# Four conditioned residual layers on one core: setup and chunk loop in one program, U kept on chip, a second gather buffer, written orders for begin and end

## What is computed

```python
# layer 0: weights made per entry, low rank (K = 30)
U = (mu @ W_dec + b_dec).reshape(B, 257, 30)       # W_dec is 128 x 7710
param = einsum('bik,kj->bij', U, V)
x = x + einsum('bsd,bde->bse', x, param[:, :-1]) + param[:, -1]
# layer 1: modulated product, demodulated, clipped
x = x + clip((x * styles) @ weight.T * dcoefs + bias, -256, 256)
# layer 2: down 256 -> 64, relu, up 64 -> 256, both scaled and shifted per entry
x = x + relu(x @ w_down) @ w_up + x
# layer 3: norms with gathered gains, three side networks, a two-layer network, a norm
h = ln(ln(x, pw_g[id], pw_b[id]), cp_g[c], cp_b[c])
t = ln(x, tm_g[c], tm_b[c]); s = ln(x, ms_g[m], ms_b[m])
cat = [w0*h, w1*t, w2*(x + mem), w3*(x + noi), w4*(x + res), w5*s]
x = x + ln(silu(cat @ W1 + b1) @ W2 + b2, g, be)
```

## Time and profile before

| | |
|---|---|
| three runs | 599.15, 596.51, 599.20 us (median 599.15) |
| the profiled execution | 592.32 us |
| its span, first to last instruction | 590.5 us |
| mean granted TensorE clock | 0.943 |
| busy: PE, DVE, ACT, POOL | 507.6, 457.5, 273.3, 395.6 us |
| moved by DMA | 69.61 MB |

### The profile page before, as it was taken

The page is one execution under the profiler, slowest core; times in us unless marked ns, Lnnn a source line. Parts: engine busy times, 40 slices in busy tenths (PEclk is TensorE's granted clock), DMA queues, the critical chain, the costliest instruction groups (busy, mean ns, idle before and its releaser), DMA issues.

```text
span 590.5 us, 8825 instructions
## 1 busy us (share of the span) xinstructions
PE 507.6 (86%) x2927; PEld 374.3 (63%) x2960; DVE 457.5 (77%) x857; ACT 273.3 (46%) x445; POOL 395.6 (67%) x382
## 2 busy tenths in 40 slices
PE   4898056569999989999989998999899999989773
PEld 3896023246676767776767676777677767757553
DVE  2579324756898979898979898989798989997543
ACT  5031010635655454647473736373737373646320
POOL 8048040878687868788777868695969697886400
PEclk9799567979999999999999999999999999999896
DMA  8954443334243525261616170708080706032011
GB/s 257 374 173 134 123 109 90 77 127 99 102 123 114 136 100 144 93 172 62 163 71 192 42 214 20 230 5 227 7 231 3 231 3 180 1 109 78 31 36 36
DMA packets 41098, 69.61 MB, mean 118 GB/s; under 512 B 5113, under 2 KB 23525, under 8 KB 40692
## 3 DMA queue, kind: packets, MB, share of 16 engines
q1 hardware_dynamic: 35732, 52.46, 32.1%
q0 software_dynamic: 5344, 16.87, 7.8%
HBM read 56.51 MB, written 12.80 MB: 117 GB/s over the span
## 4 chain that ended last, share of the span: by engine, by line
PE 46%; issue 8%; POOL 7%; DMA 4%; DVE 3%; ACT 1%; POOLq 0%; DVEq 0%; ACTq 0%
PE ps_d L773 7%; PE ps_c L739 6%; PE ps_c L740 6%; PE ps_c L741 6%; DMA pw_rows<-in_pw,gidx 4%; POOL xm_t L1141 4%; PE ps_d L782 3%; PE ps_b L739 3%; PE ps_b L740 3%; PE ps_b L741 3%; POOL x3be L1193 2%; PE ps_b L808 2%; PE ps_a L808 2%; PE ps_a L792 1%; POOL h L1168 1%
## 5 line engine op out<-in xcount | busy, mean ns | idle before, releaser
L1134 POOL DMA_INDIRECT pw_rows<-in_pw,gidx x64 | 72.4, 1131 | 27.9 <-POOL gidx L1130 13.3
L773 PE MATMUL ps_d<-xm_t,l_w 128*128 128x512 f32 x128 | 62.4, 632 | 16.0 <-POOL xm_t L1141 16.0
L1168 POOL TENSOR_TENSOR h<-xhat,pw_rows 128x1024 f32<-128x1024 f32 x16 | 38.4, 2397 | 52.4 <-DMA pw_rows<-in_pw,gidx 44.5
L1141 POOL TENSOR_TENSOR xm_t<-x_t,style 128x1024 f32<-128x1024 f32 x16 | 30.4, 1902 | 39.5 <-DVE x_t L1007 39.5
L773 PEld LDWEIGHTS ps_d<-xm_t,l_w 128*128 128x128 f32 x128 | 24.4, 201 | 43.2 <-issue 41.9
L739 PE MATMUL ps_b<-w_h,act_t_l 128*128 128x256 f32 x128 | 40.6, 317 | 9.5 <-DVE act_t_l L1091 9.5
L961 ACT ACTIVATE tm_t_h<-ps_a 128x1024 fp32r<-128x1024 f32 x16 | 16.4, 1026 | 62.5 <-DVE ps_a L1070 59.0
L984 ACT ACTIVATE ps_c<-ps_c,bias_cols 128x512 f32<-128x512 f32 x32 | 19.8, 658 | 48.6 <-PE ps_c L741 48.6
L1187 POOL TENSOR_TENSOR w_up<-w_up,ugub 128x1024 f32<-128x1024 f32 x16 | 38.2, 2385 | 1.3
L792 PEld LDWEIGHTS ps_a<-act_bd,w_up 128*128 128x128 f32 x256 | 33.6, 206 | 8.0 <-issue 4.7
L1193 POOL TENSOR_TENSOR x3be<-x,ln_gb 128x1024 f32<-128x1024 f32 x16 | 38.4, 2400 | 0.4
(11 more groups left out here) (229 smaller groups left out, 1527.1 us busy)
## 6 DMA issues: line engine op xcount, KB each, us to landing
ugub<-ugub_scratch SPq DMA_DIRECT2D x32, 512.0 KB
x_t<-in_x_t SPq DMA_DIRECT2D x16, 512.0 KB, 7.5
out<-y_out SPq DMA_DIRECT2D x16, 512.0 KB, 8.8
u_scratch<-set_u_all SPq DMA_DIRECT2D x2, 1920.0 KB
u_ch<-u_scratch SPq DMA_DIRECT2D x16, 240.0 KB, 7.9
set_wdec<-in_W_dec SPq DMA_DIRECT2D x1, 1935.0 KB, 19.5
set_wdec<-in_W_dec SPq DMA_DIRECT2D x1, 1920.0 KB, 11.3
set_w<-in_int_W SPq DMA_DIRECT2D x1, 1536.0 KB, 22.4
```

Source lines behind the costliest of these rows:

```text
L773: m = eng.matmul(ps_l1[:, o, :], l1_w[:, k, o * P:(o + 1) * P], xm_t[:, k, :], start=k == 0, stop=k == KB - 1)
L1134: eng.indirect_dma_start(pw_rows[:, j, :], None, t["pw"], bass.IndirectOffsetOnAxis(ap=gidx[:, j:j + 1], axis=0)).then_inc(s_pw, 16)
L1141: eng.tensor_tensor(by_entry(xm_t[:, :, :]), by_entry(x1_t[:, :, :]), cols(style, c), ALU.mult).then_inc(g_xm, 1)
L1168: eng.tensor_tensor(h1[:, :, :], xhat[:, :, :], pw_rows[:, :, 0:D], ALU.mult).then_inc(g_h1m, 1)
```

## The change

One program takes the place of two blocks. The setup is cut into stages of its own (`pe_dec`, `v_decode`, `act_hid`, `g_dcoef`, ...), and every engine gets three lists: `begin`, where setup stages and the stages of the first chunks are mixed in a written order, `order` with lags for the loop (again five passes of two slots, slots 6 to 15, with all lags two higher on TensorE), and `end`, the last chunks in a written order. No barrier stands between setup and loop; the first chunk's stages wait for what they need of the setup (`if first(c)`).

U stays on the chip: `u_all` is laid out [feature, half, component, entry], VectorE writes it contiguously, and a new stage `act_u` copies a chunk's part into `u_ch` in the order that `pe_t` reads. Its two writes and 16 reads of memory are gone. `pw_rows` and `gidx` have two buffers, and `g_gather` waits for `g_hadd` of two chunks before; the gather's place in the list is a slot ahead of `g_hmul`. `W_dec` is loaded first, mu sixth. W1, the nets' W2 and their rows now lie in the memory of `W_dec` and are loaded when the decode is over. The decode goes round six banks where it went round four.

```diff
-    last = max(lag for _, lag in order)
-    fill = last + 2 - last % 2
+def run_slots(eng, begin, order, end, fill):
+    for stage, n in begin:
+        stage(eng, chunk(n))
     with eng.Fori(fill // 2, NCH // 2) as i:
         for k in range(2):
+            for stage, lag in order:
+                d = k - lag
+                stage(eng, Chunk(2 * i + d, i + (d - d % 2) // 2, d % 2))
+    for stage, n in end:
+        stage(eng, chunk(n))
...
-        u_all = sb("u_all", [P, KB, B, RK])
+        u_all = sb("u_all", [P, KB, RK, B])
...
+            wdec = st("wdec", [MU, D * RK])
+            w1 = wdec[:, 0:12 * D].rearrange("p (k d) -> p k d", d=D)
+            w2n = wdec[:, 12 * D:18 * D].rearrange("p (n k d) -> p n k d", n=3, d=D)
+            rown = wdec[:, 18 * D:27 * D].rearrange("p (n m d) -> p n m d", n=3, d=D)
...
+        def load_w2n(eng, c):
+            eng.wait_ge(m_dec, NG)
+            eng.dma_start(w2n.rearrange("p n k d -> p (n k) d"), feat(t["nets_W2"])).then_inc(d_w2n, 16)
...
+        def pe_dec(eng, c):
+            g = c.n
+            k, lo, hi = GROUPS[g]
+            if lo == 0:
+                eng.wait_ge(d_front, 32)
+                eng.wait_ge(d_dec[k], 16)
+            wait(eng, v_dec, g - len(dec_bank) + 1)
+            w = wdec[:, k * P * RK:(k + 1) * P * RK].rearrange("m (i r) -> m r i", r=RK)
+            for r in range(lo, hi):
+                m = eng.matmul(dec_bank[g % 6][:, (r - lo) * B:(r - lo + 1) * B], w[:, r, :], mu, start=True, stop=True)
+            m.then_inc(m_dec, 1)
...
+        def act_u(eng, c):
+            if first(c):
+                eng.wait_ge(v_dec, NG)
+            wait(eng, p_t, c.n - 1)
+            src = u_all[:, :, :, bass.ds(c.n * CB, CB)].rearrange("p k r b -> p k b r")
+            eng.activation(u_ch[c.ring][:, :, :, :], src, ACT.Copy).then_inc(a_u, 1)
...
-            wait(eng, g_h1, c.n)
-            wait(eng, s_pw, 16 * CT * c.n)
+            wait(eng, g_h1, c.n - 1)
+            wait(eng, s_pw[c.ring], 16 * CT * c.half)
...
         @block.sync
+                      begin=[(load_dec, 0), (load_bdec, 0), (load_aw, 0), (load_l1, 0), (load_front, 0),
+                             (load_dec, 1), (load_x, 0), (load_side, 0), (load_ident, 0), (load_entry, 0),
+                             (load_bias, 0), (load_late, 0), (load_ub, 0), (load_ub, 1), (load_nets, 0),
+                             (load_ids, 0), (load_weights, 0), (load_x, 1), (load_rown, 0), (load_w2n, 0),
+                             (load_w1, 0), (load_up, 0), (load_ids, 1), (load_ub, 2), (load_up, 1), (load_ub, 3),
+                             (load_x, 2), (load_up, 2), (load_x, 3), (load_ub, 4), (load_shift, 0)],
...
         @block.tensor
+                      begin=[(pe_dec, 0), (pe_dec, 1), (pe_dec, 2), (pe_dec, 3), (pe_dec, 4), (pe_dec, 5),
+                             (pe_dec, 6), (pe_tail, 0), (pe_dec, 7), (pe_dec, 8), (pe_dec, 9), (pe_dec, 10),
+                             (pe_style, 0), (pe_dec, 11), (pe_dec, 12), (pe_dec, 13), (pe_dec, 14), (pe_dec, 15),
+                             (pe_dc, 0), (pe_hid, 0), (pe_ug, 0), (pe_t, 0), (pe_mo, 0), (pe_x1, 0), (pe_l1, 0),
+                             (pe_mot, 0), (pe_t, 1), (pe_dn, 0), (pe_row, 0), (pe_up, 0), (pe_x1, 1), (pe_x3r, 0),
+                             (pe_cls, 0), (pe_l1, 1), (pe_t, 2), (pe_xht, 0), (pe_tm, 0), (pe_dn, 1), (pe_ms, 0),
+                             (pe_up, 1), (pe_x1, 2), (pe_x3r, 1), (pe_t, 3), (pe_l1, 2)],
...
+                           (pe_x3r, 15), (pe_w2, 13), (pe_shift, 14), (pe_w1_x3, 14), (pe_w1_tm, 14),
+                           (pe_xht, 15), (pe_hht, 14), (pe_ms, 15), (pe_tm, 15), (pe_w1_ms, 14), (pe_w1_h, 14),
+                           (pe_cp, 15), (pe_w2, 14), (pe_shift, 15), (pe_w1_x3, 15), (pe_w1_tm, 15),
+                           (pe_hht, 15), (pe_w1_ms, 15), (pe_w1_h, 15), (pe_w2, 15)],
...
         @block.gpsimd
+                      begin=[(g_init, 0), (g_b2rows, 0), (g_w2low, 0), (g_dcoef, 0), (g_moroot, 0), (g_style, 0),
+                             (g_gather, 0), (g_wup, 0), (g_gather, 1), (g_style, 1), (g_rootx, 0), (g_w1mlow, 0),
+                             (g_wup, 1), (g_w1xlow, 0), (g_hmul, 0), (g_w1tlow, 0), (g_hadd, 0), (g_style, 2),
+                             (g_res, 0), (g_rootx, 1), (g_rooth, 0), (g_gather, 2), (g_wup, 2), (g_hmul, 1)],
+                      order=[(g_hadd, 5), (g_style, 3), (g_res, 5), (g_rootx, 4), (g_rooth, 5), (g_wup, 3),
+                             (g_rooty, 6), (g_gather, 3), (g_hmul, 4)],
```

More of the change, by code:

```diff
@@ L55 @@
 BRW = PIECES * CB
+GROUP = 4
+GROUPS = [(k, r, min(r + GROUP, RK)) for k in range(KB) for r in range(0, RK, GROUP)]
+NG = len(GROUPS)
 EPS = 1e-5
@@ L80, in settle, with first, chunk @@
     eng.sem_inc(sem, 1)
-def run_slots(eng, order):
-    last = max(lag for _, lag in order)
-    fill = last + 2 - last % 2
[L88 to L95, removed]
+def first(c):
+    return isinstance(c.n, int) and c.n == 0
+def chunk(n):
+    return Chunk(n, n // 2, n % 2)
@@ new lines, in conditioned_residuals, with late @@
+        nets = ((w1_mem, mu, 0, MU), (w1_nr, st_nr, 0, 64), (w1_nr, st_nr, 64, 96))
+        def late(name, shape, dt=F32):
+            return ctx.enter_context(nc.sbuf_tensor(name, shape, dt, side="right"))
+        y_out = [late(f"y_out{r}", [P, CT, D]) for r in range(2)]
+        act_t_h, act_t_l = (late(f"act_t_{e}", [P, KB, CH], F32R) for e in "hl")
+        h_t_h, h_t_l = (late(f"h_t_{e}", [P, KB, CH], F32R) for e in "hl")
+        ms_t_h, ms_t_l = (late(f"ms_t_{e}", [P, KB, CH], F32R) for e in "hl")
@@ new lines, in conditioned_residuals @@
+        tm_t_h, tm_t_l = (late(f"tm_t_{e}", [P, KB, CH], F32R) for e in "hl")
+        xh_t = late("xh_t", [P, KB, CH])
+        h1 = late("h1", [P, CT, D])
+        xhat = late("xhat", [P, CT, D])
+        x3be = [late(f"x3be{r}", [P, CT, D]) for r in range(2)]
+        x3 = late("x3", [P, CT, D])
+        x3_t_h, x3_t_l = (late(f"x3_t_{e}", [P, KB, CH], F32R) for e in "hl")
+        late("gap", [P, 13 * 32])
+        pw_rows = [late(f"pw_rows{r}", [P, CT, 2 * D]) for r in range(2)]
+        (d_front, d_bdec, d_aw, d_side, d_bias, d_l1, d_wts, d_id, d_net, d_w2n, d_rown, d_w1, d_late, d_oh, d_gain, d_cls,
+         d_ub, d_ug, d_row) = (
+            sem("d_" + n) for n in
+            "front bdec aw side bias l1 wts id net w2n rown w1 late oh gain cls ub ug row".split())
@@ new lines, in pick @@
+        def pick(eng, link, out, r1, p1, p2, p3):
+            masks = cls_const[:, 1:1 + PIECES]
+            link(eng.tensor_scalar(r1, p1, masks[:, 0:1], None, ALU.mult))
+            link(eng.scalar_tensor_tensor(r1, p2, masks[:, 1:2], r1, ALU.mult, ALU.add))
+            return eng.scalar_tensor_tensor(out, p3, masks[:, 2:3], r1, ALU.mult, ALU.add)
+        v_link = chain(nc.vector, v_chain)
+        g_link = chain(nc.gpsimd, g_chain)
+        dec_bank = [ps[:, k, :] for ps in (ps_a, ps_c, ps_d) for k in range(KB)]
```

1031 lines of the change are left out of this document (605 added, 426 removed).

## The result

The changed kernel takes 574.32 us (median, 571.79 to 575.84) against 597.83 for the kernel before: a ratio of 0.961, 95% interval 0.955 to 0.967. It is 23.5 us faster, where 45 were forecast (554, range 541 to 573). A second measurement, with the experiments, gave 572.87 and 0.9625 (0.956 to 0.969). Ratios leave out executions that ran slow as a whole at a lower granted clock; medians do not. The direction held; half of the gain is missing.

What follows compares the result with a forecast made beforehand. The loop was taken as bound by TensorE, begin and end by chains. First shift at 106.1, ten slots 280, end 160 and 1.8 around the span gave 547.9 profiled; with 6.3 of offset 554 us, range 541 to 573.

Steps and rivals of the forecast that it cites:

- W_dec and the decode: Setup: with W_dec loaded first, the decode starts at 10.5 and chunk 0's t at 46.1, against 70.66.
- The ramp, 60 us: Chunk 0's t to first shift matmul: 60 us (49.7 to 74.8), 64.9 before; idle time absorbs the moved work.
- The loop, 28.0 a slot: Ten loop slots take 280 us (278 to 283) instead of 288.85: 8.9 us saved.
- part 2: Loop: with a second gather buffer, TensorE's 9.6 us of waiting in ten slots go; 8.9 us saved.
- The copy, 0.7 us, hidden: ScalarE's copy of U takes 0.7 us (0.6 to 1.1), hidden in the loop by its wait before tm_t_h.
- The end, 160: From chunk 10's shift to the end: 160 us instead of 166.05, 6 us off (0 to 9).
- The offset, +6.3: Whole kernel: 6.3 us added to the profiled forecast of 547.9, since the shown median lay 6.8 above the profiled run.
- A: Ramp gives nothing, the moved work comes on top: first shift at 120.9, 569 us; chance 0.12.
- B: Loop: a new wait takes the gather's place, the slot stays at 28.9, 563 us; chance 0.07.
- C: Loop: strided ScalarE copy over 7.7 us makes the kernel slower, near 610 at 8.5 us; chance 0.03.
- E: Begin: nothing overlaps, load_ub holds SyncE's loads, first shift at 145.5, 599 us, no change; chance 0.03.
- D: Begin: table switches cost 1.38 us more each at three places of the chain, 558 us; chance 0.03.

Runs made afterwards that it cites:

- c4_ramp: Changed kernel with Exp early, class numbers ahead of the store, begin reordered, then GpSimd's and SyncE's orders mended: 550.75 us, ratio 0.927 to the kernel before.
- c3_ramp: Changed kernel with Exp early, class numbers ahead of the store, and the begin's first reordering (chunk 0's x1 first, GpSimd's work moved): 561.34 us, 0.942.
- d1_second_buffer: Kernel before with two gather buffers only, the gather issued at the same place but for the next chunk: 576.15 us, ratio 0.970.
- the two loop edits: On the changed kernel: ScalarE's Exp moved early in the begin, and SyncE's class number load put ahead of the store: 563.19 us, 0.949.
- b1_gather_moved: Kernel before, one gather buffer, GpSimd's gather of the next chunk moved behind rooth and ahead of w_up: 661.17 us, ratio 1.110.
- a6_gather_late: Changed kernel with Exp early and class numbers ahead of the store, one gather buffer, gather behind rooty directly before its read: 650.12 us, 1.094.

## Why the prediction was right and wrong, step by step

**W_dec and the decode: right.** Start 11.42 for 10.5, inside its 7.9 to 12.0; t(0) at 46.05 for 46.1. The run with W_dec first alone shows that the load by itself brings nothing (0 of the 5 us), which the prediction had not said; there the decode stands behind the products of the conditioning.

**The ramp, 60 us: the first of the two steps that failed.** It took 71.7 us, within the 49.7 to 74.8 given, but the value taken was wrong. The prediction said that 25.8 us of idle time would absorb the moved work. Idle time of a ramp is latency between dependent steps of one chunk, and the moved work is such a chain too: net product, statistics, root, row product, class rows. It was set between the steps of chunk 0. Three pieces can be named. The net product, the first to read weights from W_dec's old memory, waited 4.23 us for them; that one the prediction had, and gave no price of its own. Chunk 0's x1 stood behind it in TensorE's order, and its x1add behind the net's statistics in VectorE's, so xm_t(0) came late and TensorE waited 4.70 us more. GpSimd had the root of the side networks (L734) ahead of xm_t too, but that cost only 0.15 us, from 59.15 to 59.30:

```profile
55.52 1.13 PE L848 MATMUL ps_b<-t_st,v_rep 30*128 30x512 f32 x4
57.96 1.19 DVE L1163 TENSOR_TENSOR x_t<-ps_b,x_t 128x1024 f32<-128x1024 f32 x1
58.42 0.89 POOL L734 TENSOR_TENSOR set_mo_r<-set_mo_ve,mhalf 128x3 f32<-128x3 f32 x1
59.30 1.90 POOL L1321 TENSOR_TENSOR xm_t<-x_t,style 128x1024 f32<-128x1024 f32 x1
```

And VectorE's class row chain took 9.7 us instead of 3.65, with xh_t and tm(0) behind it. In the kernel after:

```profile
86.33 1.40 DVE L362 CAST set_clsb_p<-set_clsb 24x256 bf16<-24x256 f32 x1
87.76 2.47 DVE L363 TENSOR_TENSOR set_clsb<-set_clsb,set_clsb_p 24x256 f32<-24x256 f32 x1
90.26 2.32 DVE L364 CAST set_clsb_p<-set_clsb 24x256 bf16<-24x256 f32 x1
```

```profile
86.32 1.26 POOL L766 TENSOR_TENSOR w_l<-set_wdec,w_h 128x512 fp32r<-128x512 f32 x1
87.54 2.41 POOL L1369 TENSOR_TENSOR w_up<-up_rep,ugub 128x1024 f32<-128x1024 f32 x1
90.03 2.40 POOL L1371 TENSOR_TENSOR w_up<-w_up,ugub 128x1024 f32<-128x1024 f32 x1
```

In c4_ramp the same subtraction takes 0.41:

```profile
81.82 0.41 DVE L363 TENSOR_TENSOR set_clsb<-set_clsb,set_clsb_p 24x256 f32<-24x256 f32 x1
```

Each slow VectorE instruction begins 0.01 to 0.23 us behind a GpSimd one and ends 0.15 to 0.28 us after it. The Trainium skill (SBUF — State Buffer, Who interferes with whom) says that VectorE with two SBUF inputs or in a two-port mode contends with GpSimd for the one port pair that they share, "an exclusive lock", held for the instruction. The rows agree: instructions of 0.28 and 0.41 us last as long as the GpSimd instruction of 2.4 us beside them. No run changes one piece alone, but c3_ramp's trace parts them (3.1 us by chunk 0's x1 and 4.5 by the class row chain, at tm(0)), and c4_ramp has them together, 12.5 us at the first shift (9.4 in the other profile with its orders). From chunk 0's t that ramp takes 57.8 us: the forecast's 60 could be had, and what failed was to take it as given by this order.

**The loop, 28.0 a slot: right for part 2, wrong for the whole, the second step that failed.** The gather's wait went, and d1_second_buffer shows 27.8 a slot with nothing in its place. What failed is that the step looked at GpSimd's and VectorE's work alone. ScalarE's table loads (1.28 us each, in the earlier trace rows as a cost of the begin) were not asked about at the loop's entry, and the new order of SyncE, with idx_ch behind the store and 1.5 MB, was not walked at all, though the prediction named which loads stand behind which in the begin. Together they cost 11.6 us in ten slots (291.9 to 280.3), 7.9 by the second profile of the changed kernel, and 9.7 by the medians.

**The copy, 0.7 us, hidden: size wrong, conclusion right.** It takes 1.05 to 1.07, at the upper end, and doubling it changes nothing in the loop. VectorE's adds did shrink, as the prediction allowed: 0.69 us each, written contiguously, for 1.13.

**The end, 160: 162.8.** 2.3 us are one wait for x of chunk 14, behind ugub in SyncE's written end. The prediction read two waits of w2 for act_t_l in the earlier trace rows, but there were three; the last chunk's own stands behind them, and it is the one that is left:

```profile
576.07 0.58 PE L739 MATMUL ps_b<-w_h,act_t_l 128*128 128x256 f32 x1 [3.25 <-DVE act_t_l L1091]
```

In the kernel after, the two of the earlier trace rows, 6.26 us together, have become one of 0.97 at 537.98, beside a new one of 1.69 us for ms_t_l, and the last chunk's, at 557.38, is 3.26. So the written end took what it aimed at, and the wait for x of chunk 14 gave part of it back.

**The offset, +6.3:** the profiled execution of the kernel after lies 0.3 us above its median where that of the kernel before lay 5 to 7 below. The profiles alone are 17.7 us apart, the medians 23.5. The forecast for a profiled run was 547.9 and 574.6 came, 26.7 us off, where the median was 20.3 off: this term hid 6 us of the error, by luck.

**The rivals.** A (the ramp gives nothing: first shift at 120.9, 569 us) was nearest in the ramp, 3 us from what came. B named 28.9 us a slot, and 29.2 came; but its mechanism, GpSimd's new order, is not the cause: with that order kept and the two loop edits made, a slot takes 28.0. Each was held to be rare with the other absent, and the upper end of 573 was A with a little of the loop. That A and B could both happen, 578 us by their prices, was left out of the range, and the result is 1.3 us outside it. C and E did not come. D (1.38 us more for a table switch) neither. In the kernel after:

```profile
43.48 1.28 ACT L658 ACT_TABLE_LOAD   x1
44.77 0.42 ACT L658 ACTIVATE set_dm<-set_dm 128x256 f32<-128x256 f32 x1
45.20 1.28 ACT L664 ACT_TABLE_LOAD   x1
46.50 1.66 ACT L664 ACTIVATE set_hid<-ps_c,bias_cols 128x128 f32<-128x128 f32 x6
```

The Trainium skill (ScalarE: Activation LUTs, What ACT_TABLE_LOAD costs) adds 1.38 us of draining to each switch; in these rows the gap on either side of a load is 0.01 to 0.02 us, and the measurement decides.

## What to carry to other kernels

Idle time in a ramp is room only for an order that fits it: before work is laid into it, write the chain of each of the two and see whose steps wait for whose, in every engine's order, SyncE's too. A loop that is entered with another activation table than its last pass leaves pays for it in every pass, and a small load behind 1.5 MB of others in the DMA list came 12 us after its issue. Where two arrivals meet at one wait, removing either shows little: remove both before judging one. And measure each part of a large change alone: here the second buffer by itself gave most of what the whole change gave.

## What the runs showed of the hardware that was not expected

The clock adds to a wait. TensorE's slots at full clock have 27.8 us of work; in slots with a wait of 4.5 us in one place (b1_gather_moved, all slots from the second on) the granted clock is 0.95 and the same work takes 29.5. Within such a slot the clock falls around the wait, which ends at 278.34, and is 1.00 again from 282 on:

```profile
264.20:275.00 10.80, 9.61 (x45) 6.60 (x44) 8.54 (x16) 4.12 (x7) 9.37 (x6) 1.00 0.35 97
275.00:282.00 7.00, 3.66 (x14) 3.29 (x15) 5.32 (x9) 2.46 (x4) 4.99 (x5) 0.76 0.70 157
```

The slot of 32.35 us in the kernel after has 29.6 at 0.95, against 28.1.

A load of 18 KB issued behind 1.5 MB took 12.17 us to land. A gather took 6.2 us from its last issue to its read in the earlier trace rows, and 9.5 us with x and ugub issued between its issues (a6_gather_late, at 266.27); no run shows that they are the cause.
